# Cross attention and feed-forward block on one Trainium2 core: the first group's queries in two halves over two banks, fewer warm-up products, and weight rows cleared by ScalarE

## What is computed

```python
# attention: x (64,64,128) queries, ctx (64,64,256) keys and values, one mask for both
src_trans = (einsum('bsf,of->bso', ctx, W_src) + b_src) * mask[:, :, None]
tgt_trans = (einsum('btf,of->bto', layernorm(x), W_tgt) + b_tgt) * mask[:, :, None]
k, v = split(src_trans); q = tgt_trans            # 8 heads of 16
attn = softmax(where(mask == 0, -inf, q k^T / 4))
x = x + einsum(concat(layernorm(x), attn v), W_out) + b_out
# feed-forward: fq() rounds each block of 16 to the grid 0, .5, 1, 1.5, 2, 3, 4, 6 times its scale
h = silu(fq(layernorm(x)) fq(w_gate)^T) * (fq(layernorm(x)) fq(w_up)^T)
x = x + fq(h) fq(w_down)^T
```

## Time and profile before

| | us |
|---|---|
| median of 3 runs | 198.53 |
| lowest and highest of them | 198.27, 199.17 |
| the profiled execution, its own time | 198.98 |
| its span, first to last instruction | 196.8 |
| around the span (198.98 - 196.8) | 2.2 |

### The profile page before, as it was taken

One profiled execution on the slowest core, in us unless ns is written; L12 is line 12 of the kernel. 1 busy time (PEld: TensorE's weight loads), 2 busy tenths in 40 slices (PEclk: granted clock), 3 DMA queues, 4 the chain that ended last, 5 costly groups with the idle time before them and its releaser, 6 DMA issues.

```text
span 196.8 us, 5874 instructions
## 1 busy us (share of the span) xinstructions
PE 185.5 (94%) x2117; PEld 143.2 (73%) x2117; DVE 179.8 (91%) x402; ACT 130.2 (66%) x276; POOL 138.9 (71%) x205
## 2 busy tenths in 40 slices
PE   8998979999999999999998999689999998999985
PEld 8764765968859678597686877367777776777884
DVE  6779897899999999999979998999999989999992
ACT  3115969959878689697777954475566483666661
POOL 6324495567598997884937587697999975886770
PEclk9999999999999999999999999999999999999999
DMA  5889308840020000000000000000102010101005
GB/s 182 253 226 337 143 8 250 278 161 12 12 98 2 3 3 3 2 0 5 3 0 3 3 2 0 3 2 2 53 0 57 0 53 0 56 3 53 2 3 160
DMA packets 13698, 11.99 MB, mean 61 GB/s; under 512 B 790, under 2 KB 10590, under 8 KB 13670
## 3 DMA queue, kind: packets, MB, share of 16 engines
q1 hardware_dynamic: 13086, 11.23, 18.6%
q10 hardware_dynamic: 584, 0.39, 0.7%
HBM read 9.52 MB, written 2.10 MB: 59 GB/s over the span
## 4 chain that ended last, share of the span: by engine, by line
PE 35%; POOL 30%; issue 18%; DVE 12%; ACT 3%; POOLq 1%; DVEq 0%; ACTq 0%
POOL wq_y L403 8%; POOL hq L418 8%; PE bank L1090 5%; PE bank L1187 4%; POOL xn L290 3%; POOL sch L410 3%; DVE mx L730 3%; PE bank L1078 3%; PE a_pair L1041 2%; PE bank L1053 2%; PE bank L1041 2%; PE bank L1027 2%; PE bank L1084 2%; POOL rs L280 2%; DVE st L691 2%
## 5 line engine op out<-in xcount | busy, mean ns | idle before, releaser
L1181 PE MATMUL bank<-wdT,hT 128*128 128x128 f32 x186 | 26.4, 278 | 1.0 <-ACT hT L636 0.7
L1146 PE MATMUL bank<-guT,xqT 128*128 128x352 f32 x64 | 24.5, 464 | 1.8 <-DVE hh L895 1.8
L1181 PEld LDWEIGHTS bank<-wdT,hT 128*128 128x128 f32 x186 | 23.2, 191 | 2.4 <-ACT hT L636 1.4
L1149 PE MATMUL bank<-guT,xqT 128*128 128x352 f32 x64 | 24.2, 460 | 0.0
L403 POOL TENSOR_TENSOR wq_y<-hh,ivh 128x704 f32<-128x704 f32 x15 | 21.1, 1408 | 3.0 <-ACT ivh L642 2.3
L418 POOL TENSOR_TENSOR hq<-wq_u,sch 128x704 f32<-128x704 f32 x14 | 19.8, 1415 | 3.6 <-DVE wq_u L921 3.5
L748 DVE TENSOR_REDUCE den<-prob 128x8 f32<-128x512 f32 x32 | 19.8, 666 | 0.0
L522 ACT ACTIVATE k_bd<-bank,bk_of,head_of 128x512 f32<-128x512 f32 x16 | 12.4, 780 | 10.2 <-PE bank L1078 10.2
L1090 PE MATMUL bank<-wsT,cT 128*128 128x128 f32 x128 | 17.3, 279 | 0.5 <-DVE q_m L722 0.4
L636 ACT COPY hT<-bank 128x384 f32<-128x384 f32 x32 | 15.2, 475 | 3.7 <-PE bank L1161 3.6
L1161 PEld LDWEIGHTS bank<-ident,hq 128*128 128x128 f32 x96 | 11.9, 141 | 7.5 <-issue 3.0
(11 more groups left out here) (141 smaller groups left out, 510.6 us busy)
## 6 DMA issues: line engine op xcount, KB each, us to landing
cT<-in_ctxT SPq DMA_DIRECT2D x8, 512.0 KB, 5.7
x_all<-in_x SPq DMA_DIRECT2D x8, 256.0 KB, 6.0
mask_bc<-in_mask_rows SPq DMA_DIRECT2D x8, 256.0 KB, 5.7
out_y<-mask_bc SPq DMA_DIRECT2D x7, 256.0 KB, 2.3
wsT<-in_WsT ACTq DMA_DIRECT2D x1, 256.0 KB, 4.8
out_y<-x_all SPq DMA_DIRECT2D x1, 192.0 KB, 2.0
w_all<-in_wg SPq DMA_DIRECT2D x1, 176.0 KB
w_all<-in_wu SPq DMA_DIRECT2D x1, 176.0 KB
```

Source lines behind the costliest of these rows:

```text
L1146: nc.tensor.matmul(gu_bank[2 * n % 3][:, 0:I], xqT[g % 2][:, t], guT[:, 0, :], start=True, stop=True).then_inc(pe_g, 1)
L1149: nc.tensor.matmul(gu_bank[(2 * n + 1) % 3][:, 0:I], xqT[g % 2][:, t], guT[:, 1, :], start=True, stop=True).then_inc(pe_u, 1)
L1181: last = nc.tensor.matmul(bank[:, j * P:(j + 1) * P], hT[n % 2][:, c, :], wdT[:, c, :], start=(c == 0), stop=(c == 2))
```

## The change

The front warm-up has 42 products instead of 62. The four transposes of group 0 go two by two to the first halves of two banks, `w0` and `o_bank`; each pair is copied by DVE as a half of 256 columns, projected by PE as a half, and masked by DVE as a half, with semaphores of their own for the first half (`pe_xh`, `xh_ok`, `pe_qh`, `qh_ok`). The two clears of `w_all` move from DVE to ACT, as copies from `calm`, between ACT's tiny exponential and its last four mask loads.

```diff
+        pe_xh, xh_ok, pe_qh, qh_ok = sem("pe_xh"), sem("xh_ok"), sem("pe_qh"), sem("qh_ok")
+        halves, half_bank = (slice(0, GT // 2), slice(GT // 2, GT)), (w0, o_bank)
...
             nc.scalar.activation(warm[:, :], minus_half[:, :], ACT.Exp)
+            act.wait_ge(calm_ok, 1)
+            nc.scalar.copy(w_all[64:P, 0:WBLK, :], calm[64:P, 0:BLK].unsqueeze(1).to_broadcast([P - 64, WBLK, BLK])
+                           ).then_inc(w_zero, 1)
+            nc.scalar.copy(w_all[:, WBLK + NB_H:WALL, :], calm[:, 0:BLK].unsqueeze(1).to_broadcast([P, WALL - WBLK - NB_H, BLK])
+                           ).then_inc(w_zero, 1)
...
             normalise1(0)
-            nc.vector.memset(w_all[64:P, 0:WBLK, :], 0.0).then_inc(w_zero, 1)
-            nc.vector.memset(w_all[:, WBLK + NB_H:WALL, :], 0.0).then_inc(w_zero, 1)
-            dve.wait_ge(pe_xnT, 1)
-            nc.vector.tensor_copy(xnT[0][:, :], w0[:, :]).then_inc(xnT_ok, 1)
+            for h in range(2):
+                dve.wait_ge(pe_xnT if h else pe_xh, 1)
+                nc.vector.tensor_copy(xnT[0][:, halves[h]], half_bank[h][:, 0:GT // 2]).then_inc(xnT_ok if h else xh_ok, 1)
+            dve.wait_ge(ld_m[0], 16)
+            dve.wait_ge(ld_b, 16)
+            for h in range(2):
+                dve.wait_ge(pe_q if h else pe_qh, 1)
+                nc.vector.scalar_tensor_tensor(out=q_m[0][:, halves[h]], in0=half_bank[h][:, 0:GT // 2], scalar=b_q,
+                                               in1=mask_bc[:, halves[h]],
+                                               op0=ALU.add, op1=ALU.mult).then_inc(qm_ok if h else qh_ok, 1)
...
-                if on(g1):
+                if on(g1) and k > 0:
                     q_masked(g1)
...
+                if g == 0:
+                    pe.wait_ge(qh_ok, 1)
                 pe.wait_ge(qm_ok, g + 1)
...
+            def first_transpose(h):
+                pe.wait_ge(xn_ok, 1)
+                for j in range(2):
+                    last = nc.tensor.transpose(half_bank[h][:, j * P:(j + 1) * P], xn[0][:, 2 * h + j, :], ident[:, :])
+                last.then_inc(pe_xnT if h else pe_xh, 1)
+
+            def first_queries(h):
+                pe.wait_ge(ld_wt, 16)
+                pe.wait_ge(xnT_ok if h else xh_ok, 1)
+                nc.tensor.matmul(half_bank[h][:, 0:GT // 2], wtT[:, :], xnT[0][:, halves[h]],
+                                 start=True, stop=True).then_inc(pe_q if h else pe_qh, 1)
...
-            warm_up(62)
+            warm_up(42)
...
                     k_project(0)
-                    xn_transpose(0)
+                    first_transpose(0)
+                    first_transpose(1)
                     warm_up(8)
-                    q_project(0)
+                    first_queries(0)
+                    first_queries(1)
                     warm_up(10)
```

More of the change, by code:

```diff
@@ L718, in q_masked @@
                 dve.wait_ge(ld_m[g], 16)
-                if g == 0:
-                    dve.wait_ge(ld_b, 16)
                 past(dve, pe_s, g - 1)
```

## The result

| | before | changed |
|---|---|---|
| median of 4 runs, us | 198.40 | 196.09 |
| lowest and highest | 198.25, 199.17 | 195.95, 196.42 |
| the profiled execution, own time | 198.98 | 196.42 |
| its span | 196.8 | 194.3 |

The ratio of the changed kernel to the one before is 0.9877, 95% interval 0.9854 to 0.9900.

What follows compares the result with a forecast made beforehand. The opening up to the first scores at 12.38 us was taken as one serial chain. Terms -0.79 and -0.72 made -1.51; with a gain of 1.1 to 1.5, 198.53 - 1.25 gave 197.3 us, range 196.8 to 199.2.

Steps and rivals of the forecast that it cites:

- the last of the sum: After the first scores: the opening's whole shift of -1.51 us lasts to the end, 198.98 to 197.47 us.
- 42 warm-ups: Kernel front: keys' product starts near 6.05 instead of 7.19, transposes at 8.17 instead of 8.96, -0.79 us.
- The trace disagrees: PE's opening: matmul rate doubled after 5.8 us of activity, against about 4 us in the Trainium skill.
- Halves: Transposes to first scores: copies, queries' product and masking in two halves bring scores to about +2.7 from +3.42, -0.72 us.
- Clears on ACT: DVE loses a memset of 0.91 us that would delay the first half copy; nothing more counted; ACT takes at most 1.45.
- the margin: SP's queue: x of group 1 lands at 10.37, 0.4 us before DVE's statistics of group 1 need it.
- Splitting pays little: Rival on the opening's half operations: they save only 0.15 to 0.35 us, total 197.6 to 198.0; chance 0.31 including DVE swallowing shift.
- The clock stays low: Rival on PE's opening: the pause from 5.46 to 6.05 keeps 1.2 GHz, total 198.8 to 201.0; chance 0.14, 0.11 slower.
- The change does nothing: Rival on the keys' start: context or `wsT` lands at about 7.2, only the split queries count, 197.8 us; chance 0.03.

## Why the prediction was wrong, step by step

**The step that failed** is the last of the sum: "Behind it every step is released by engines, not by a clock or a load, so I let the shift run to the end". A step can wait for one thing more: PE stopped at a fixed number of its own instructions, most likely for the next block of them. Before, this cost 1.0 us on the path in group 0's weighted values, and the 20 warm-ups less took that away: 1.15 of the 2.56 us between the two profiles. I had read the trace of the first 20 us only, and costed the warm-ups by their time, never by their number. The stop stood in the list of waits, as an idle time of PE released by "issue".

**42 warm-ups, -0.79 predicted, -0.72 measured** (transposes at 8.24 for 8.96), with two errors that cancel. The key weights landed 5.2 us after their issue, not 4.8, so the keys started at 6.45 and not 6.05, behind a pause of 0.81. And the four passes took 1.79 us, all at the high rate: the clock rose in the pause, while I had the first pass slow and took 2.12. Both are this execution's. In the six other profiles with 42 warm-ups and the key weights issued as here, these landed 4.6 to 5.0 us after their issue and the transposes started at 7.72 to 8.08. In one of the six, with 15 tiny products, the first pass was in part slow as I had it, 0.71 us against 0.50 in the changed kernel. The clock's rise at 6.75, 5.8 us after the first product, was one execution's too: in five other profiles it came 3.3 to 3.9 us after it, and in the last six not within the 42 or 20 warm-ups. So my "The trace disagrees" rested on a single execution.

**Halves, -0.72 predicted, -0.51 measured.** Counted from the first transpose, the copies started at +0.42 and the queries' product at +0.99, as predicted. The two copies took 0.76, so a half costs about 0.4 as interpolated. But the first masking started at +1.81 instead of +1.66, the second ended at +2.69 instead of +2.57, and the scores started at +2.91 instead of +2.7. On PE the four passes and their tail took 0.94 us up to the ten warm-ups, and these 0.66, where I had 0.88 and 0.56.

**Group 1.** Another 0.17 came where nothing was predicted: its normalising on DVE took 1.34 us instead of 1.51. Beside it on POOL runs the preparation of the mask (1.69 us); the two overlapped for 0.64 us before and 0.47 after. The other profiles bear the link out: in eleven of the twelve the normalising took its overlap with that operation (0.47 to 0.87 us) and 0.86 or 0.87 more. In the twelfth the overlap was 0.06 and the normalising took 1.19. No run moved the one without the other.

**Clears on ACT, counted at nothing but as a cover: right in kind, mis-sized.** They took 1.04 and 0.22 us and ended at 5.97, the weight loads went out at 5.99. Taken back, they cost 0.61, not the 0.3 expected: that 0.3 counted from a first copy at 8.66, and with the transposes at 7.81 it was due at 8.23.

**Loads.** x of group 1 landed at 10.37 again, and the statistics began at 10.85: the margin held here. It is thin: with whole queries beside ACT's clears the load came at 11.4 and was waited for. Of SP's later loads the next six went out 1.4 to 3.1 us earlier; the last of them took 2.60 us to issue, and those behind it went out later than before (13.52 for 12.42 with a context load).

**The rivals.** *Splitting pays little*: wrong, it pays 0.85 beside the clears on ACT. *The clock stays low*: did not happen with a pause of 0.8 us, but the mechanism is real, as the run with 20 warm-ups shows. *The change does nothing*: wrong. No rival had a gain beyond the opening, and so the range ended at 196.8 where 196.1 was measured.

**The profile against the median.** I guessed that an earlier rise of the clock shortens the old opening; the 62 warm-ups of 5.36 us show that it does. The changed kernel waits for its weights instead, and its runs lie within 0.5 us.

## What to carry to other kernels

Warm-up products on TensorE have two costs: the time for which they hold back work whose data are there, and the instructions that they put ahead of everything behind them. Where PE stops within a row of like products and nothing releases it, count its instructions to that point, look for an instruction packet some 2.5 us before the end of the stop and for like stops a fixed number of instructions further on, and try fewer or wider products ahead. Parts of a change that look like one term each can depend on each other, so test them in all pairs before pricing one.

## What the hardware showed that was not expected

- PE stopped for 0.84 to 1.18 us at its 346th product, give or take one, in four profiles of four programs, though the products ahead differed in size and time. An instruction packet moved 2.3 to 2.6 us before the end each time. Smaller stops stood at the 470th and the 722nd or 723rd. What stays open is why the stop can be absent with as many products ahead: in the one profile that shows this, of the changed kernel with 62 warm-ups, the packet came at 21.5 instead of 24.1 to 25.5. The times suggest the same for one more of its ten executions and for two of ten with 25 late tiny products.
- With 42 warm-ups, all at the low rate, and a pause of 0.81 us, the keys ran at the high rate from their first pass (0.43 us from one to the next). With 20 warm-ups and a pause of 2.60 us they ran at the low rate throughout.
- Moving one 256 KB load 0.47 us ahead, on another queue, to the moment at which a second 256 KB load is issued, made the second land 1.1 us later: 4.1 us after its issue, where it took 2.9 to 3.1 in the eleven other profiles.
- DVE's normalising of group 1 (four operations of 128 columns) took 1.34 to 1.74 us in eleven of the twelve profiles, by how long POOL's 1.69 us of mask preparation ran beside it, and each 0.1 us of overlap went with 0.1 us of length.
